# A recurrence over 64 steps: the state kept in the store of states, and both passes written out with constant places

## What is computed

```python
def step(carry, xs):
    h, c = carry
    i_t = sigmoid(xi_t + h @ V_i); f_t = sigmoid(xf_t + h @ V_f)   # f_t is not used
    g_t = tanh(xg_t + h @ V_c);    o_t = sigmoid(xo_t + h @ V_o)
    c_new = h * c + i_t * g_t
    h_new = o_t * tanh(c_new)
    return (h_new, c_new), h_new
# out = t + hs, t being the tokens
```

## Time and profile before

| | us |
|---|---|
| median of 3 runs | 2313.25 (2313.23 to 2313.42) |
| the profiled execution | 2311.74 |
| its span in the profile | 2310.0 |
| first pass, first to last L1668 of s = 0 | 1896.31 to 2076.25 |
| second pass, the same | 2081.22 to 2262.96 |
| last stage, from its first copy | 2278.06 to 2310.0 |

### The profile page before, as it was taken

The page is one execution under the profiler, slowest core; times in us unless marked ns, Lnnn a source line. Parts: engine busy times, 40 slices in busy tenths (PEclk is TensorE's granted clock), DMA queues, the critical chain, the costliest instruction groups (busy, mean ns, idle before and its releaser), DMA issues. The chain is left out here.

```text
span 2310.0 us, 48136 instructions
## 1 busy us (share of the span) xinstructions
PE 1809.4 (78%) x11055; PEld 1560.1 (68%) x11055; DVE 1462.4 (63%) x6045; ACT 1220.1 (53%) x3165; POOL 1149.5 (50%) x1812
## 2 busy tenths in 40 slices
PE   6967799867655432999999993776995569999995
PEld 5956688864443332999999993446983358887884
DVE  6965899967867541444444443993228977777776
ACT  5765999944434301656556562542006666665554
POOL 5856777731777773555555555884006620001220
PEclk9989999985555555999999996887556769999998
DMA  4022444421222342222222223547833100000003
GB/s 151 0 74 61 124 120 123 122 77 44 85 81 66 127 98 66 76 74 77 75 76 74 78 60 101 179 157 123 152 65 88 55 5 0 0 0 1 0 0 147
DMA packets 247357, 178.00 MB, mean 77 GB/s; under 512 B 93191, under 2 KB 213317, under 8 KB 247244
## 3 DMA queue, kind: packets, MB, share of 16 engines
q1 hardware_dynamic: 229836, 142.71, 23.5%
q0 software_dynamic: 17408, 34.00, 4.5%
HBM read 123.76 MB, written 54.97 MB: 77 GB/s over the span
## 5 line engine op out<-in xcount | busy, mean ns | idle before, releaser
L1523 POOL DMA_INDIRECT choices<-y,small x288 | 286.1, 993 | 226.8 <-ACT y L1553 156.6
L1205 POOL DMA_INDIRECT sorted_tokens<-work x256 | 248.7, 972 | 139.4 <-issue 77.4
L1586 PEld LDWEIGHTS banks<-w,hidden 128*128 128x128 f32 x2304 | 268.1, 192 | 5.5
L1586 PE MATMUL banks<-w,hidden 128*128 128x128 f32 x2304 | 268.5, 275 | 0.0
L1636 PEld LDWEIGHTS banks<-small 128*128 128x128 f32 x1536 | 192.8, 191 | 64.8 <-issue 31.9
L1636 PE MATMUL banks<-small 128*128 128x128 f32 x1536 | 225.2, 283 | 13.4 <-ACT small L1670 9.1
L377 PE MATMUL banks<-ident,small 128*128 128x128 f32 x640 | 120.3, 306 | 122.7 <-ACT small L364 77.2
L1717 POOL COPY work_again<-small 128x128 f32 x128 | 37.9, 296 | 352.2 <-DVE small L1700 352.2
L1627 PE MATMUL banks<-ab_tiles,small 128*128 (+1 forms) x768 | 209.6, 383 | 1.2 <-DVE small L1900 1.2
L1553 ACT ACTIVATE y<-y,small 128x128 f32<-128x128 f32 x288 | 92.3, 391 | 196.4 <-DVE y L1494 196.4
L377 PEld LDWEIGHTS banks<-ident,small 128*128 128x128 f32 x640 | 78.7, 160 | 150.2 <-issue 66.7
(11 more groups left out here) (261 smaller groups left out, 4574.7 us busy)
## 6 DMA issues: line engine op xcount, KB each, us to landing
small<-L_conv_protein_pair SPq DMA_DIRECT2D x128, 256.0 KB
rows<-sorted_tokens SPq DMA_DIRECT2D x72, 262.0 KB, 2.8
work_again<-choices SPq DMA_DIRECT2D x32, 512.0 KB, 3.7
work_again<-L_conv_protein_pair SPq DMA_DIRECT2D x32, 512.0 KB, 7.5
x_tiles<-x SPq DMA_DIRECT2D x32, 256.0 KB, 3.6
work<-x SPq DMA_DIRECT2D x32, 256.0 KB, 2.9
after_mixture<-x_tiles SPq DMA_DIRECT2D x32, 256.0 KB, 2.2
work_again<-after_mixture SPq DMA_DIRECT2D x32, 256.0 KB, 2.7
```

Of the source, the lines that this page charges most:

```text
L1205: pool.indirect_dma_start(out=self.sorted, out_offset=bass.IndirectOffsetOnAxis(ap=where[:, u // BATCH, u % BATCH * G + t, k:k + 1], axis= ...
L1523: pool.indirect_dma_start(out=self.out, out_offset=bass.IndirectOffsetOnAxis(ap=where[:, u, t:t + 1], axis=0), in_=y[:, u % 4, t, :], in_o ...
L1586: last = pe.matmul(out[:, t * P:(t + 1) * P], hidden[:, u % 2, h, t * P:(t + 1) * P], w2[:, u % 2, h * P:(h + 1) * P], start=h == 0 and t ...
```

## The change

Each new h is written once, straight into the store: `state(step + 1, s)` is the slot of that step and half, `state(0, s)` the start states. TensorE and `forget` read h from there. `cell.h` goes, and with it Pool's copies, the `saved` flow and the increment L1699; Pool has no part in the stage any more. For the first and second pass (`written`) all 64 steps are written out on TensorE, VectorE and ScalarE, with constant places and constant wait values; the third keeps a loop, of six turns, with the first and last eight steps written out. The first pass writes into the store too. TensorE's increment of `paced_pe` in `finish` remains only in the third pass, now also ahead of half 0's matmuls. At the end of a pass two copies take the last h of each half into `end_h`, where `begin` and `compare` read it (`closed`); `begin` copies c in two halves and no h. `WARM` was 64, so the first pass had 64 steps before as well.

```diff
...
     def each_step(self, eng, stage):
-        with eng.Fori(self.first // UNROLL, STEPS // UNROLL) as i:
+        head = STEPS if self.written else UNROLL
+        for step in range(head):
+            stage(step, step % 2)
+        if self.written:
+            return
+        with eng.Fori(1, STEPS // UNROLL - 1) as i:
             for u in range(UNROLL):
-                step = i * UNROLL + u
-                stage(step - self.first if self.first else step, step, u % 2)
+                stage(i * UNROLL + u, u % 2)
+        for step in range(STEPS - UNROLL, STEPS):
+            stage(step, step % 2)
     def tensor(self, pe, base, base_h):
...
-        def finish(k, par, s):
-            self.stepped.ready(pe, base_h + (k * HALVES + s))
+        def finish(step, par, s):
+            self.stepped.ready(pe, base_h + (step * HALVES + s))
+            if not self.written:
+                pe.sem_inc(cell.paced_pe, 1)
             if s > 0:
-                self.read.ready(pe, base + (k * HALVES + (s - 1)))
-                pe.sem_inc(cell.paced_pe, 1)
+                self.read.ready(pe, base + (step * HALVES + (s - 1)))
+                if not self.written:
+                    pe.sem_inc(cell.paced_pe, 1)
             for g in range(len(GATES)):
...
-                last = pe.matmul(cell.sums(par, g)[:, s, :], cell.v_w[:, g, :], cell.h[:, 1 - par, s, :], start=False,
+                last = pe.matmul(cell.sums(par, g)[:, s, :], cell.v_w[:, g, :], cell.state(step, s), start=False,
...
+        def body(step, par):
+            finish(step, par, 0)
+            more = not isinstance(step, int) or step < STEPS - 1
+            if more:
+                self.read.free(pe, base + ((step + 1) * HALVES + (HALVES - 1)))
+                prime(step + 1, 1 - par, (0, 1))
+            finish(step, par, 1)
+            if more:
+                prime(step + 1, 1 - par, (2,))
         self.read.free(pe, base + (HALVES - 1))
-        prime(0, self.first, 0, (0, 1, 2))
-        with pe.Fori(self.first // UNROLL, STEPS // UNROLL - 1) as i:
-            body(i, False)
-        body(STEPS // UNROLL - 1, True)
+        prime(0, 0, (0, 1, 2))
+        self.each_step(pe, body)
...
-                if self.stores:
-                    self.saved.free(dve, n)
-                    dve.sem_inc(cell.paced, 1)
-                self.stepped.done(dve.tensor_tensor(cell.h[:, par, s, :], o, cell.g[:, s, :], ALU.mult))
-        forget(0, 0, 0)
-        with dve.Fori(self.first // UNROLL, STEPS // UNROLL - 1) as i:
-            for u in range(UNROLL):
-                stage(i * UNROLL + u - self.first if self.first else i * UNROLL + u, u % 2, False)
-        for step in range(STEPS - UNROLL, STEPS):
-            stage(step - self.first, step % 2, step == STEPS - 1)
-    def gpsimd(self, pool, base, base_h):
-        cell = self.cell
-        if not self.stores:
-            return
-        def stage(k, step, par):
-            for s in range(HALVES):
-                self.stepped.ready(pool, base_h + (k * HALVES + (s + HALVES)))
-                self.saved.done(pool.tensor_copy(cell.hs[:, bass.ds(step + s * STEPS, 1), :].rearrange("p a n -> p (a n)"),
-                                                 cell.h[:, par, s, :]))
-        self.each_step(pool, stage)
+                self.stepped.done(dve.tensor_tensor(cell.state(step + 1, s), o, cell.g[:, s, :], ALU.mult))
+        forget(0, 0)
+        self.each_step(dve, stage)
+        for s in range(HALVES):
+            self.stepped.ready(dve, base_h + (STEPS * HALVES + s))
+            dve.sem_inc(cell.paced, 1)
+            self.closed.done(dve.tensor_copy(cell.end_h[:, s, :], cell.state(STEPS, s)))
...
-        dve.tensor_copy(self.ends()[1], cell.start[:, 1, :])
         for s in range(HALVES):
-            self.stepped.done(dve.tensor_copy(cell.h[:, 1, s, :], cell.start[:, 0, s * P:(s + 1) * P]))
-    def ends(self):
-        cell = self.cell
-        return (cell.h[:, 1, :, :].rearrange("p s n -> p (s n)"), cell.c.rearrange("p s n -> p (s n)"))
+            self.stepped.done(dve.tensor_copy(cell.c[:, s, :], cell.start[:, 1, s * P:(s + 1) * P]))
...
+    def state(self, step, s):
+        if isinstance(step, int) and step == 0:
+            return self.start[:, 0, s * P:(s + 1) * P]
+        return self.hs[:, bass.ds(step + (s * STEPS - 1), 1), :].rearrange("p a n -> p (a n)")
+    def ends(self):
+        return self.end_h.rearrange("p s n -> p (s n)"), self.c.rearrange("p s n -> p (s n)")
...
-        warm = Pass(cell, "warm", STEPS - WARM, False)
-        main = Pass(cell, "main", 0, True)
-        more = Pass(cell, "more", 0, True)
+        warm, main, more = (Pass(cell, tag, tag != "more") for tag in ("warm", "main", "more"))
...
-            @block.gpsimd
-            def _(pool):
-                main.saved.open(pool)
-                more.saved.open(pool)
-                main.gpsimd(pool, 0, 0)
-                rounds(pool, lambda t: more.gpsimd(pool, t * per, t * per_h))
...
```

More of the change, by code:

```diff
@@ L26 @@
 CHUNK_TOL = 2.0 ** -18
-WARM = 64
 def engine_loop(eng, total, unroll, stages, peel=0):
@@ L1598, with __init__ @@
 class Pass:
-    def __init__(self, cell, tag, first, stores):
-        self.cell, self.first, self.stores = cell, first, stores
-        self.steps = STEPS - first
+    def __init__(self, cell, tag, written):
+        self.cell, self.written = cell, written
         chip = cell.chip
@@ L1639, in finish, with stage @@
                     self.summed.done(last)
-        def body(i, last):
-            for u in range(UNROLL):
[L1643 to L1652, removed]
+        def body(step, par):
[7 more added lines that the diff above has]
+                prime(step + 1, 1 - par, (2,))
         self.read.free(pe, base + (HALVES - 1))
-        prime(0, self.first, 0, (0, 1, 2))
-        with pe.Fori(self.first // UNROLL, STEPS // UNROLL - 1) as i:
-            body(i, False)
-        body(STEPS // UNROLL - 1, True)
+        prime(0, 0, (0, 1, 2))
+        self.each_step(pe, body)
     def scalar(self, act, base):
         cell, banks = self.cell, self.cell.chip.banks
-        def stage(k, step, par):
+        def stage(k, par):
             for s in range(HALVES):
@@ L1676, in vector, with forget, stage @@
         cell = self.cell
[L1678 to L1683, removed]
+        def forget(step, s):
+            self.stepped.ready(dve, base_h + (step * HALVES + s))
+            dve.tensor_tensor(cell.hc[:, s, :], cell.state(step, s), cell.c[:, s, :], ALU.mult).then_inc(self.links, 1)
+        def stage(step, par):
             for s in range(HALVES):
-                n = base + (k * HALVES + s)
+                n = base + (step * HALVES + s)
                 g, i, o = (cell.open[:, s, gate, :] for gate in range(3))
@@ L1692, in stage @@
                 if s == 0:
-                    forget(k, par, 1)
-                elif not last:
-                    forget(k + 1, 1 - par, 0)
+                    forget(step, 1)
+                elif not isinstance(step, int) or step < STEPS - 1:
+                    forget(step + 1, 0)
                 self.bounded.ready(dve, n)
-                if self.stores:
-                    self.saved.free(dve, n)
-                    dve.sem_inc(cell.paced, 1)
-                self.stepped.done(dve.tensor_tensor(cell.h[:, par, s, :], o, cell.g[:, s, :], ALU.mult))
-        forget(0, 0, 0)
-        with dve.Fori(self.first // UNROLL, STEPS // UNROLL - 1) as i:
-            for u in range(UNROLL):
-                stage(i * UNROLL + u - self.first if self.first else i * UNROLL + u, u % 2, False)
-        for step in range(STEPS - UNROLL, STEPS):
-            stage(step - self.first, step % 2, step == STEPS - 1)
-    def gpsimd(self, pool, base, base_h):
-        cell = self.cell
-        if not self.stores:
-            return
-        def stage(k, step, par):
-            for s in range(HALVES):
-                self.stepped.ready(pool, base_h + (k * HALVES + (s + HALVES)))
-                self.saved.done(pool.tensor_copy(cell.hs[:, bass.ds(step + s * STEPS, 1), :].rearrange("p a n -> p (a n)"),
-                                                 cell.h[:, par, s, :]))
-        self.each_step(pool, stage)
+                self.stepped.done(dve.tensor_tensor(cell.state(step + 1, s), o, cell.g[:, s, :], ALU.mult))
[5 more added lines that the diff above has]
+            self.closed.done(dve.tensor_copy(cell.end_h[:, s, :], cell.state(STEPS, s)))
     def begin(self, dve, fresh, base_h):
@@ L1727, in begin @@
         else:
[L1728 removed]
+            ends = cell.ends()
             cell.chain(dve.tensor_copy(cell.start[:, 0, 1:CHUNKS], ends[0][:, 0:CHUNKS - 1]))
             cell.chain(dve.tensor_copy(cell.start[:, 1, 1:CHUNKS], ends[1][:, 0:CHUNKS - 1]))
[L1731 removed]
         for s in range(HALVES):
[L1733 to L1737 removed]
+            self.stepped.done(dve.tensor_copy(cell.c[:, s, :], cell.start[:, 1, s * P:(s + 1) * P]))
 class Links:
@@ L1804, in __init__ @@
```

(12 more changed lines are left out.)

4 lines of the change are left out of this document (2 added, 2 removed).

## The result

| | us |
|---|---|
| before, median of 4 runs | 2313.24 (2308.54 to 2313.42) |
| after, median of 4 runs | 2288.19 (2283.09 to 2291.57) |
| ratio | 0.9879, 95% interval 0.9847 to 0.9911 |
| profiled execution after | 2291.57, span 2289.8 |

The account below looks back on a forecast made before the run. TensorE's gapless stream was taken to bound the first pass, VectorE's in-order ring the second. 14.6 + 12.1 - 0.8 = 25.9 us off the profiled 2311.74 gave 2285.8, plus 1.51 for the median: 2287.3 us, range 2280 to 2297.

Parts of the forecast that it names:

- VectorE's ring: VectorE's in-order chain from one write of h to the next: 1.42 us a half in the second pass, falling to 1.26.
- Second pass, 14.6 us: Wait and increment before the write of h go, and the loop turns; 181.74 falls to 167.1 us, 14.6 gained.
- First pass, 12.1 us: Seven table loads go (10.6 us) and steps fall from 2.683 to 2.653; 179.94 to 167.8 us, 12.1 gained.
- the 2.653 for 125 intervals: Step time in us forecast for the first and second pass once written out, taken from eight already written-out steps.
- the eight steps: Last eight steps of the first pass before the change, TensorE and VectorE already written out, 2.653 us each.
- TensorE's lost increment: TensorE's `sem_inc` dropped in each second `finish`: taken as worth 0, lower bound 0, upper bound 16 us.
- Seams, 0.8 us lost: At pass ends and the second pass's start: added `end_h` copies cost 1.0 us, fewer start copies return 0.2.
- The jump, 0 (bounds -1 to 2): Jump past the unrun third pass to the last stage, 7.1 us before: no change forecast, bounds -1 and +2.
- A: Both passes: straight code is not delivered fast enough; mild form 2296 us, chance 0.06, harsh form 2339, chance 0.03.
- B: Second pass: write of h stays late through its dependence on two engines, step stays 2.824; 2298 us, chance 0.04.
- C: First pass: table loads stay, placed by something other than the loop; 10.6 us less gain, 2298 us, chance 0.02.
- D: Both passes: TensorE's increments space its stream; step 2.52, 16 us more gain, 2271 us, or half, 2279; chance 0.05.

Follow-up runs that it names:

- a5_inc_dve: The changed kernel with VectorE's increment of `paced` put back before the write of h, all passes; passes 173.56 and 172.56 us, single run 2300.76 us.
- a8_second_wait: The changed kernel with a second, long met wait before the write of h, no increment; passes 170.19 and 169.20 us, single run 2294.50 us.
- b1_written: The kernel before with only its first and second pass written out, Pool's copies, wait and increment kept; 2291.37 us, ratio 0.9923.
- a2_swapped: The changed kernel with TensorE's two waits ahead of half 1 in the other order, written-out passes only; 2281.92 us, ratio to the kernel before 0.9856.
- a4_loops: The changed kernel with all three passes in the third's looped form, h still written straight into the store; 2333.55 us, ratio to the kernel before 1.0113.
- a0_after: The changed kernel, unaltered, run again on another chip beside the version with swapped waits; 2284.20 us, ratio to the kernel before 0.9874.

## Why the prediction was right, point by point

*Where the time was.* Held: the second pass was bound by VectorE's ring, and with that eased, TensorE's side is what is left, at 2.683 us a step against the ring's 2 x 1.27. It is not its stream alone, though: of the 2.683, 0.03 is the late weight load.

*Second pass, 14.6 us.* Measured 12.56. The mechanism held in the main: the delay ahead of the write went, most of its 0.14 us is the increment's (0.12 by the rows of `a5_inc_dve`), and a second wait, long met, costs nothing (`a8_second_wait`). But the difference of 2.824 and 2.653 was not all this delay, as the prediction had it, and that Pool's copies cost nothing by themselves was wrong for the kernel before: there L1691 takes 351 ns beside them, and 292 without them. The 0.141 us from 2.824 to 2.683 are made up of three terms: 0.053 for the loops, most likely through those stretched instructions, and 0.118 for the store through Pool (both from `b1_written`), less 0.030 for the two waits of TensorE in their worse order (`a2_swapped`). How the 0.118 divides between the increment, the wait on Pool and the copies was not taken apart; the increment alone, on the kernel after, costs 0.05.

*First pass, 12.1 us.* Measured 9.97. Seven table loads left with 1.52 us each, 10.6, as forecast; the first interval grew by 0.31 (3.29 to 3.60; it lies between 3.42 and 4.00 in the other profiles, and its cause is open). The steps stayed at 2.683, where 2.653 was forecast. That the loads need no written-out pass to vanish is shown by `a4_loops`: with eight written-out steps ahead of its loop it has only the load at the entry.

The Trainium skill ("ScalarE: Activation LUTs", What ACT_TABLE_LOAD costs) would have seven loads give back 18.6 us, by a figure that it states for a switch to a different set of functions, while these loads brought back the set that was there; the 9.97 measured speaks for the rows' 1.52 each.

*The mis-sized term* is thus the 2.653 for 125 intervals: (2.683 - 2.653) x 125 = 3.8 us. The prediction called the eight steps "the changed form in all but ScalarE's loop", and priced TensorE's lost increment at 0 with the lower bound 0, "for nothing is added to TensorE". Taking it out left the two waits in the order in which the weight load starts late, and cost those 3.8 us, which `a2_swapped` gives back without it: 1.17 + 1.75 us against `a0_after`, and 0.58 more that its longer first interval (4.00 against 3.42) takes away, 3.5 in all.

*Seams, 0.8 us lost.* Measured 5.19 - 4.97 = 0.22 between the passes and 0.02 behind the second, 0.2 in all. The two copies take 0.46 us of time, as forecast. That they hardly show behind the second pass is probably because its last step lies behind the 63 intervals and loses its delay there too, which the sum left out; this was not tested.

*The jump, 0 (bounds -1 to 2).* Measured -1.56, beyond the bound. Pool's leaving is not the cause, since `b1_written` has Pool in the stage and 5.68. All eleven other profiles have 5.3 to 5.8, and only the one of the kernel before 7.08; what made that one long stays open. That kernel has a single profile, so the 7.08 may be of that execution alone.

*Rivals.* A, code not delivered: in both its forms out for the changed kernel, whose intervals from the second to the last have no outlier above 2.69 us inside a pass but the one of 2.82 at the start of the second; the instruction queues carried 57 and 78 packets (44 and 69 before). The Trainium skill ("Runtime: NRT & Kernel Launch", Instruction fetch mechanics), by which a straight stream is fetched ahead, agrees with that. B: out, the delay left with the increment. C: out, one load is left. D: out, for the step is no shorter without TensorE's increment; it is 0.03 longer, by the order of the waits.

The sum of the measured terms, -9.97 - 12.56 + 0.22 + 0.02 - 1.56 and -0.14 at the entry (from the stage's first memset to the first sigmoid, 4.07 before and 3.93 after), is -24.0 us, against -25.9 forecast. Without the jump, which was not forecast and whose cause is open, it is -22.4, short of the forecast by 3.5, about what the order of the waits cost. The profiled execution shows 20.2, for the stages ahead took 3.8 us more in it; the medians show 25.05. That they come within 1 us of the forecast is in part luck: the jump made up for 1.6 us, the terms were 2 us off even so, and the stages ahead wander by more.

## What to carry to other kernels

A change of two halves must be priced in both orders: here writing out gave 0.8% alone, the direct store in loops cost 1.1% (with the increments of that form on TensorE), and together they gave 1.2%. VectorE's write of h started 0.14 to 0.17 us behind the tanh with its place in a register, and 0.03 with a constant one; for TensorE the place and the increments were not told apart. Where a stretch of the kernel before already has the changed form, take its rate, but compare the streams wait by wait first: two waits ahead of one matmul in the other order were worth 0.03 us a step. An engine for which nobody waits can still cost time: look whether its work stretches the neighbour's instructions. And the loop that reloaded ScalarE's table at each turn was mended here by one turn written out ahead of it.

## What was not expected of the hardware

Of two waits ahead of a matmul group, one stood in a record of its own and one on the weight load. With the later signal on the record of its own the load started 0.11 us behind that signal and 0.06 ahead of its matmul, and from the first of the six matmuls to the next group it was 0.72 us; with the later signal on the load itself it was 0.05, 0.12 and 0.67. A weight load of such a group with its operand at a place in a register, in the form of the loop here with its increments, started 0.55 us after the last signal that it needs, against 0.05 to 0.11 with constants. VectorE's write at a place in a register started 0.14 to 0.17 us behind its signal, against 0.03. An increment between a wait and VectorE's instruction delays that instruction by 0.12 us (0.15 against 0.03), while a second, met wait delays it by nothing.

Pool's copies and VectorE's small instructions slow each other, and which of them pays depends on the time. In the kernel before nearly every copy started up to 0.12 us ahead of L1691, kept its 293 ns and stretched L1691, to 316 to 410 ns. In `b1_written` the copies started 0.17 to 0.31 us ahead of L1699, which kept its 291 ns, and the earlier ones took up to 0.43 us themselves.
